# Causal attention in five steps a quad of heads instead of six

## The chip, the cores and the metric

One core of a Trainium2 chip runs the whole program. The metric is the device time of one execution in microseconds (us); the kernel before has a median of 998.64 us over three runs (998.04 to 999.71). Engines: PE is TensorE (PEld its weight loads), DVE VectorE, ACT ScalarE, POOL GpSimd, SP SyncE, which only issues DMAs here.

## The reference, cut to what matters

`x` has 4 sequences of 512 positions with 128 features. Six sub-layers follow one another, and attention, in 16 heads of 8, is part of four of them:

```
x = x + 0.5 * L0_ffn(layernorm(x))    # full attention, then the best of 8 experts
x = x + L0_attn(layernorm(x))         # causal attention
x = x + 0.5 * L0_ffn(layernorm(x))    # the same weights again
x = x + 0.5 * L1_ffn(layernorm(x))    # two dense low-rank-corrected experts
x = x + L1_attn(layernorm(x))         # causal attention
x = x + 0.5 * L1_ffn(layernorm(x))
```

An attention is softmax(q k^T / sqrt(8) + mask) v for each head, then a projection. In the causal ones a position sees itself and those before it, so of the 4 x 4 blocks of 128 x 128 scores of a head ten are needed, four of them masked along the diagonal. All of it is fp32 in the reference.

## The kernel before, in words

A *batch* here is one attention of one sequence: 16 of them, 0 to 3 and 8 to 11 full, 4 to 7 and 12 to 15 causal. A batch has four *quads* of four heads. Each quad is handled in two passes over its scores. `p1` (TensorE, L594, stationary q, moving k; for the diagonal blocks also mask products, L600) writes scores into a pair of PSUM banks, and VectorE takes the negated maximum of every row of every block (`blockm`, L948) and, after the last chunk, of every row (`negm`, L953). On POOL `split` (L1225 to L1231) writes that maximum as three bf16 parts. `m` (TensorE, L650) transposes them, ScalarE copies them out (`mrow`, L785), and two DMAs that SyncE issues (L1276) put them as extra rows into the stacked q, so that `p2` (L594 again, stationary k, moving q) computes score minus maximum. ScalarE writes the exponentials to `pt` (L795), and `pv` (TensorE, L675, fp32: each product is two records) multiplies them by the values and adds up in one bank. After every second quad `evac` (ScalarE, L801) copies that bank out, and `o` (L683) transposes it; after the fourth `onT` (L688) and `out` (L693) project the batch.

A *step* `(c, t)` is one chunk `c` of the scores for pair `t` of the quad's heads; the two heads of a pair (`s`) have a bank each. A causal quad has three chunks. c0 has the four diagonal blocks, c1 four full ones, c2 the two that are left: 512, 512 and 256 columns a head. So the six steps, 0 to 5, are (0,0), (0,1), (1,0), (1,1), (2,0), (2,1).

PSUM: two pairs of banks in turn for the "A" jobs (`p1`, `v`, `o`, `out`, ...), three banks in a ring for the "B" jobs (`p2` takes two of them, `hT`, `q`, `k`, `m`, `onT`, ... one each), and bank 7 for `pv`. A `p2` waits until every B bank taken before it but the last has been read; another B job until all but the last two have; an A job until all A jobs but the last have. `pt` is a ring of eight steps.

All engines run through one plan in order, made by `segment`, for three segments: batches 0 to 3, 4 to 11, 12 to 15. It goes through the steps of the second pass (a *slot* each). In a slot there come: the *jobs* whose time has come, counted in quads (so a slot of a causal quad begins at a sixth); what is due by slots; the first pass of the quad two ahead (`LEAD`); `p2`. Before the first quad two quads' `p1` alone are the segment's lead. After the last `p1` of a quad come `split` and, `M_LATER` = 4 slots later, `m`. After the second pair's `p2` of a chunk, `pv` is due `V_LATER` = 2 slots later for its first half (`VALUES`), 3 for its second. `evac`, `o`, `onT` and `out` are due 3, 5, 7 and 9 slots after a quad's last step. The jobs are the preparation of later batches (`PREP`, in quads before the batch: `hT` 6.967, `q` 6.767, `k` 6.486, `v` 2.951, with layer norm and remainders), the DMAs that stack the bf16 parts of q and k (`STACK`), and feed-forward work.

## Time and profile before

| | |
|---|---|
| runs | 998.04, 998.64, 999.71 us |
| profiled execution, span | 996.2 us |
| its own time | not listed apart; the runs' median is 2.4 us above its span |
| TensorE busy | 890.2 us (89%) |
| VectorE busy | 759.1 us (76%) |
| ScalarE busy | 674.5 us (68%) |
| GpSimd busy | 331.3 us (33%) |
| mean granted TensorE clock | 0.974 |
| causal batches 4 to 7 begin (their first `p2`) | 328.93 us |
| causal maxima (L948), first and last | 316.8 and 930.9 us |

The span is what lies between the first and the last instruction of one profiled execution; the runs' times have a little around it. The causal parts are about the slices 13 to 19 and 33 to 39 of the page's 40. A busy TensorE isn't one at its peak, since ends of products are modelled and products overlap.

### The profile page before, as it was taken

How to read it: one execution, taken by the hardware profiler on the slowest of the kernel's cores; microseconds unless marked ns; L12 is line 12 of the kernel's file. 1: busy time of each engine (PE TensorE's matmuls, PEld its weight loads, DVE VectorE, ACT ScalarE, POOL GpSimd, SP SyncE). 2: the span in 40 equal slices, each digit the busy share in tenths (PEclk: the TensorE clock that was granted, in tenths of full speed). 3: DMA queues.
4: the chain of work that ended last, by engine and by line, in shares of the span. 5: the costliest groups of instructions: out<-in, count | busy, mean ns of one | idle time of the engine just before them, and what ended most of it. 6: DMA issues, size and time to landing. Idle time of an engine off the chain costs nothing.

```text
span 996.2 us, 25709 instructions
## 1 busy us (share of the span) xinstructions
PE 890.2 (89%) x10020; PEld 474.5 (48%) x10020; DVE 759.1 (76%) x1352; ACT 674.5 (68%) x1470; POOL 331.3 (33%) x603
## 2 busy tenths in 40 slices
PE   2699999898888899999999998889798989999998
PEld 1123333235877455554323333249685545555565
DVE  5889999873536887888999999916347888888646
ACT  2388887687666677777798877786462367777631
POOL 4454312241655323332232412416651132311101
PEclk9699999999989999999999999999899999999999
DMA  4117740010133211111111100010310222110000
GB/s 145 51 35 189 189 108 13 16 34 22 39 112 107 63 51 43 46 51 40 34 45 31 44 18 2 24 42 31 98 57 1 64 66 57 43 38 5 3 22 22
DMA packets 60521, 52.32 MB, mean 53 GB/s; under 512 B 9106, under 2 KB 57362, under 8 KB 60402
## 3 DMA queue, kind: packets, MB, share of 16 engines
q1 hardware_dynamic: 48980, 40.00, 14.9%
q10 hardware_dynamic: 8478, 4.62, 2.1%
q0 software_dynamic: 2944, 6.05, 1.9%
q8 instruction: 81, 1.33, 0.6%
q14 instruction: 38, 0.31, 0.1%
HBM read 13.64 MB, written 11.06 MB: 25 GB/s over the span
## 4 chain that ended last, share of the span: by engine, by line
PE 57%; DVE 20%; ACT 10%; issue 7%; POOL 3%; DMA 2%; ACTq 1%; DVEq 0%; POOLq 0%; SPq 0%
PE ps L594 14%; PE ps L675 14%; DVE negm L957 10%; ACT pt L795 8%; PE ps L740 5%; PE ps L724 4%; PE ps L733 4%; DVE blockm L948 3%; PE ps L600 3%; PE ps L630 3%; PE ps L746 2%; PE ps L683 2%; PE ps L693 2%; PE ps L635 2%; DVE l_stats L992 1%
## 5 line engine op out<-in xcount | busy, mean ns | idle before, releaser
L795 ACT ACTIVATE pt<-ps 128x512 f32<-128x512 f32 (+1 forms) x896 | 458.2, 566 | 151.6 <-PE ps L594 101.5
L957 DVE TENSOR_REDUCE negm<-ps 128x2 f32<-128x1024 f32 x256 | 300.7, 1219 | 27.5 <-PE ps L594 25.5
L675 PE MATMUL ps<-pt,va 128*32 128x256 f32 (+1 forms) x4352 | 273.9, 340 | 11.8 <-ACT ot L801 5.0
L948 DVE TENSOR_REDUCE blockm<-ps 128x8 f32<-128x1024 f32 (+1 forms) x192 | 194.6, 1042 | 31.4 <-PE ps L594 20.1
L594 PE MATMUL ps<-ks,qs 61*128 61x128 bf16 (+2 forms) x1536 | 172.6, 291 | 31.4 <-DVE negm L957 17.3
L594 PE MATMUL ps<-qs,ks 64*128 64x128 bf16 (+3 forms) x1408 | 167.9, 295 | 6.1 <-ACT pt L795 2.0
L675 PEld LDWEIGHTS ps<-pt,va 128*32 128x32 f32 x4352 | 91.9, 108 | 125.0 <-issue 80.8
L594 PEld LDWEIGHTS ps<-ks,qs 61*128 61x128 bf16 x1536 | 54.5, 95 | 184.4 <-issue 85.6
L1225 POOL CAST mpart<-negm 128x16 bf16<-128x16 f32 x64 | 13.3, 209 | 296.3 <-DVE negm L957 153.6
L829 ACT ACTIVATE stage<-ps,pt 128x128 f32<-128x128 f32 x240 | 68.7, 371 | 30.5 <-PE ps L724 29.5
L594 PEld LDWEIGHTS ps<-qs,ks 64*128 64x128 bf16 x1408 | 57.9, 94 | 59.7 <-ACT pt L795 45.1
L1165 POOL TENSOR_TENSOR q<-q,parts 128x512 f32<-128x512 f32 x29 | 33.6, 1159 | 111.8 <-ACT parts L777 111.8
L724 PE MATMUL ps<-hTm,pt 128*128 128x128 f32 x480 | 67.6, 286 | 3.3 <-ACT stage L829 1.3
L733 PE MATMUL ps<-experts,stage 128*128 x480 | 65.1, 279 | 2.3 <-DVE pt L1077 2.2
L1077 DVE TENSOR_TENSOR pt<-ps,pt 128x128 f32<-128x128 f32 x60 | 17.2, 287 | 64.4 <-PE ps L733 63.3
L724 PEld LDWEIGHTS ps<-hTm,pt 128*128 128x128 f32 x480 | 61.4, 200 | 6.4 <-ACT stage L829 3.4
L733 PEld LDWEIGHTS ps<-experts,stage 128*128 128x128 f32 x480 | 59.0, 194 | 3.6 <-issue 3.4
L740 PE MATMUL ps<-hTa,wk 128*128 128x512 f32 x128 | 58.5, 599 | 0.9 <-ACT hTa L818 0.8
L1069 DVE COPY pt<-experts 128x644 f32 x60 | 32.1, 535 | 25.6 <-PE ps L675 23.5
L835 ACT ACTIVATE stage<-ps 128x512 f32<-128x512 f32 x32 | 19.1, 598 | 38.9 <-PE ps L740 37.5
L1260 POOL DMA_INDIRECT y_rows<-pt,stage x30 | 30.2, 1008 | 35.6 <-DVE pt L1077 29.0
L1089 DVE TENSOR_SCALAR stage<-ps,wpk 128x512 f32<-128x512 f32 x32 | 23.9, 747 | 22.9 <-PE ps L740 22.9
(150 smaller groups left out, 1062.7 us busy)
## 6 DMA issues: line engine op xcount, KB each, us to landing
qs<-parts SPq DMA_DIRECT2D x80, 128.0 KB
ks<-parts SPq DMA_DIRECT2D x77, 128.0 KB
experts<-in_experts SPq DMA_DIRECT2D x8, 578.0 KB, 5.5
sorted<-stage ACTq DMA_DIRECT2D x4, 967.5 KB, 8.4
qs<-mrow SPq DMA_DIRECT2D x128, 6.0 KB
pt<-y_rows SPq DMA_DIRECT2D x8, 256.0 KB, 3.1
qs<-parts SPq DMA_DIRECT2D x32, 56.0 KB
ks<-parts SPq DMA_DIRECT2D x30, 56.0 KB
```

Of the source, the lines that this page charges most:

```text
L594: ends[s] = pe.matmul(banks[s][:, col:col + c1 - c0], stationary[s][:, i * P:(i + 1) * P], moving[s][:, c0:c1], start=(m_ == 0), stop=(not ...
L675: ins = pe.matmul(pv_bank[32 * j:32 * j + 32, q0:q1], va[n % 2][:, kb, value_at(g, j):value_at(g, j) + 32], pt[:, k_, from_:from_ + q1 - q ...
L724: ins = pe.matmul(b_tiles(o)[:, a, :], we[:, number_of(n, at) % NWE, a * P:(a + 1) * P], hTm[:, number_of(n, at) % 2, :], start=True, stop ...
L733: ins = pe.matmul(pair_of(ka)[:, 0, 0:P], mid_e[:, number_of(n, at) % 2, a, :], w2.rearrange("p o c -> p (o c)"), start=(a == 0), stop=(a ...
L740: pe.matmul(pair_of(ka)[:, 0, :] if kx else b_bank(o), wk[:, kx, at * P:(at + 1) * P], hTa[:, n % 2, :], start=True, stop=True).then_inc(a ...
L795: a.activation(pt[:, k_ % NPT, S * s:S * s + width], b_bank(o + s)[:, 0:width], ACT.Exp).then_inc(b_free, 1)
L829: ins = a.activation(mid_e[:, number_of(n, at) % 2, fb, :], b_tiles(o)[:, fb, :], ACT.Relu, bias=we[:, at_, F + fb:F + fb + 1])
L948: v.tensor_reduce(blockm[:, g % 2, :, t, PLACES[c_]], pair_of(ka)[:, :, 0:width].rearrange("p s (b c) -> p s b c", c=P), AX, ALU.max, nega ...
L957: v.tensor_reduce(negm[:, g % 2, :, t, c_], pair_of(ka), AX, ALU.max, negate=True).then_inc(a_free, 1)
L1069: v.tensor_copy(we[:, number_of(n, at) % NWE, :], experts[:, bass.ds(expert[n, at], 1), 0:WE] .rearrange("p o c -> p (o c)")).then_inc(lai ...
L1165: eng.tensor_tensor(q32[:, c_, :], q32[:, c_, :], parts[:, c_, 0, :], ALU.subtract).then_inc(rem_done[c_], 1)
L1260: g_.indirect_dma_start(d["y_rows"][n], bass.IndirectOffsetOnAxis(sorted_rows[n % 2][:, at, P:ROW] .bitcast(U32), 0), ysb[:, r, :], None). ...
```

## The change

The last causal chunk, c2, is handled once for both pairs: the scores of pair 1 stand beside those of pair 0 in the same two banks, 256 columns further (`SHARED`). A causal quad has the steps (0,0), (0,1), (1,0), (1,1), (2,BOTH), in both passes. The maximum of the last is taken of the full 1,024 elements in one instruction, its exponentials of 512 columns in each of two, and its value products are one call of 256 columns instead of two of 128. A slot is a fifth of a causal quad; `M_LATER`, `V_LATER` and all job times keep their numbers. `evac`, `o`, `onT` and `out` are due 2, 4, 6 and 8 slots after a causal quad's last step, since the last value call has no second half. Full batches keep their eight steps. The diff, without the places that only pass both pairs' q and k on or look up the last step:

```diff
@@ -63,12 +63,15 @@
            [(0, 0, P, S), (2, 3 * P, 3 * P, S)],
            [(1, 0, 2 * P, S)]],
 }
+BOTH = 2
+STEPS = {False: [(c, t) for c in range(TB) for t in range(2)], True: [(0, 0), (0, 1), (1, 0), (1, 1), (2, BOTH)]}
+SHARED = 2 * P
 
 VALUES = {
     False: [[[(kb, 0, 0, S // 2)], [(kb, S // 2, S // 2, S)]] for kb in range(TB)],
     True: [[[(kb, kb * P, kb * P, (kb + 1) * P) for kb in (0, 1)], [(kb, kb * P, kb * P, (kb + 1) * P) for kb in (2, 3)]],
            [[(0, 0, P, 3 * P)], [(0, 2 * P, 3 * P, S), (2, 3 * P, 3 * P, S)]],
-           [[(1, 0, 2 * P, 3 * P)], [(1, P, 3 * P, S)]]],
+           [[(1, 0, 2 * P, S)]]],
 }
 
 PLACES = [slice(0, 16, 5), slice(11, 15), slice(7, 10, 2)]
@@ -189,8 +192,8 @@
 def segment(batches, causal_of, jobs):
 
     quads = [(n, g) for n in batches for g in range(4)]
-    nstep = [2 * len(PASS1[causal_of[n]]) for n, _ in quads]
-    pass1 = [(n, g, c, t) for n, g in quads for c in range(len(PASS1[causal_of[n]])) for t in range(2)]
+    nstep = [len(STEPS[causal_of[n]]) for n, _ in quads]
+    pass1 = [(n, g, c, t) for n, g in quads for c, t in STEPS[causal_of[n]]]
     jobs = list(jobs)
     for k, n in enumerate(batches):
         if k == 0:
@@ -221,22 +224,24 @@
             n, g, c, t = pass1[done1]
             out.append(("p1", n, (g, c, t)))
             done1 += 1
-            if (c, t) == (len(PASS1[causal_of[n]]) - 1, 1):
+            if (c, t) == STEPS[causal_of[n]][-1]:
                 out.append(("split", n, g))
                 due.append((slot + M_LATER, "m", n, g))
         if own:
             Q, i = own
             n, g = quads[Q]
-            out.append(("p2", n, (g, i // 2, i % 2)))
-            if i % 2:
-                for half in range(2):
-                    due.append((slot + V_LATER + half, "pv", n, (g, i // 2, half)))
+            c, t = STEPS[causal_of[n]][i]
+            out.append(("p2", n, (g, c, t)))
+            if t:
+                for half in range(len(VALUES[causal_of[n]][c])):
+                    due.append((slot + V_LATER + half, "pv", n, (g, c, half)))
                 if i == nstep[Q] - 1 and g % 2:
-                    due.append((slot + V_LATER + 1, "evac", n, g // 2))
-                    due.append((slot + V_LATER + 3, "o", n, g // 2))
+                    last = V_LATER + len(VALUES[causal_of[n]][c]) - 1
+                    due.append((slot + last, "evac", n, g // 2))
+                    due.append((slot + last + 2, "o", n, g // 2))
                     if g == 3:
-                        due.append((slot + V_LATER + 5, "onT", n, None))
-                        due.append((slot + V_LATER + 7, "out", n, None))
+                        due.append((slot + last + 4, "onT", n, None))
+                        due.append((slot + last + 6, "out", n, None))
         slot += 1
     at = len(quads)
     while due or jobs:
@@ -585,14 +592,16 @@
 
             return VW * (8 * (g % 2) + 4 * (g // 2) + j)
 
-        def score_pieces(pe, pieces, diagonal, banks, stationary, moving, mask):
+        def score_pieces(pe, pieces, diagonal, t, banks, stationary, moving, mask):
 
 
             ends = [None, None]
-            for m_, (i, col, c0, c1) in enumerate(pieces):
+            pieces = [(u, i, col + SHARED * u * (t == BOTH), c0, c1) for u in ((0, 1) if t == BOTH else (t,))
+                      for i, col, c0, c1 in pieces]
+            for m_, (u, i, col, c0, c1) in enumerate(pieces):
                 for s in range(2):
-                    ends[s] = pe.matmul(banks[s][:, col:col + c1 - c0], stationary[s][:, i * P:(i + 1) * P],
-                                        moving[s][:, c0:c1], start=(m_ == 0),
+                    ends[s] = pe.matmul(banks[s][:, col:col + c1 - c0], stationary[s][:, u, i * P:(i + 1) * P],
+                                        moving[s][:, u, c0:c1], start=(m_ == 0),
                                         stop=(not diagonal and m_ == len(pieces) - 1), skip_group_check=True)
             for half in range(2 if diagonal else 0):
                 for s in range(2):
...
                 elif name == "pv":
                     g, c_, half = at
                     odd, pieces = g % 2, VALUES[w["causal"]][c_][half]
                     need(pe, a_free, at_a[("v", n, None)] + 1)
-                    need(pe, b_free, at_b[("p2", n, (g, c_, 1))] + 2)
+                    shared = (c_, BOTH) in STEPS[w["causal"]]
+                    need(pe, b_free, at_b[("p2", n, (g, c_, BOTH if shared else 1))] + 2)
                     if not odd and c_ == 0 and half == 0:
                         need(pe, pv_free, at_evac[(n, g // 2)])
                     for m_, (kb, col, q0, q1) in enumerate(pieces):
                         begins = not odd and c_ == 0 and half == 0 and m_ == 0
                         ends_ = odd and ev == final_pv(n, g) and m_ == len(pieces) - 1
                         for j in range(4):
-                            k_ = at_step[("p2", n, (g, c_, j // 2))] % NPT
-                            from_ = S * (j % 2) + col
+                            k_ = at_step[("p2", n, (g, c_, BOTH if shared else j // 2))] % NPT
+                            from_ = S * (j % 2) + SHARED * (j // 2) * shared + col
                             ins = pe.matmul(pv_bank[32 * j:32 * j + 32, q0:q1],
                                             va[n % 2][:, kb, value_at(g, j):value_at(g, j) + 32],
                                             pt[:, k_, from_:from_ + q1 - q0], start=begins, stop=bool(ends_),
@@ -789,7 +799,7 @@
                     need(a, x_moe, 8 if n >= 12 else 4 if n >= 4 else 0)
                     if k_ >= NPT:
                         need(a, pv_done, pv_of_step[k_ - NPT] + 1)
-                    width = max(col + q1 - q0 for _, col, q0, q1 in PASS2[w["causal"]][c_])
+                    width = SHARED * (t == BOTH) + max(col + q1 - q0 for _, col, q0, q1 in PASS2[w["causal"]][c_])
                     for s in range(2):
                         need(a, b_full, o + s + 1)
                         a.activation(pt[:, k_ % NPT, S * s:S * s + width], b_bank(o + s)[:, 0:width],
@@ -944,10 +954,14 @@
                     g, c_, t = at
                     need(v, m_parts, 4 * (at_quad[(n, g)] - 1))
                     if w["causal"]:
-                        width = max(col + k1 - k0 for _, col, k0, k1 in PASS1[True][c_])
-                        v.tensor_reduce(blockm[:, g % 2, :, t, PLACES[c_]],
-                                        pair_of(ka)[:, :, 0:width].rearrange("p s (b c) -> p s b c", c=P), AX, ALU.max,
-                                        negate=True).then_inc(a_free, 1)
+                        if t == BOTH:
+                            v.tensor_reduce(blockm[:, g % 2, :, :, PLACES[c_]],
+                                            pair_of(ka).rearrange("p s (t b c) -> p s t b c", t=2, c=P), AX, ALU.max,
+                                            negate=True).then_inc(a_free, 1)
+                        else:
+                            v.tensor_reduce(blockm[:, g % 2, :, t, PLACES[c_]],
+                                            pair_of(ka).rearrange("p s (b c) -> p s b c", c=P), AX, ALU.max,
+                                            negate=True).then_inc(a_free, 1)
                         if ev == final_p1(n, g):
                             need(v, a_free, ka + 1)
                             v.tensor_reduce(negm[:, g % 2].rearrange("p s t i -> p (s t i)"),
```

## Rows read from the trace of the kernel before

**Rows 1.** Groups by line and form, 345 to 460 us: busy us, mean ns | idle before.

```profile
L948 DVE TENSOR_REDUCE blockm<-ps 128x8 f32<-128x1024 f32 x49 | 58.8, 1221 | 7.8 <-PE ps L594 3.9 <-POOL mpart L1225 1.7 <-PE ps L600 1.2
L948 DVE TENSOR_REDUCE blockm<-ps 128x4 f32<-128x512 f32 x26 | 17.7, 690 | 6.9 <-PE ps L594 6.7
```

**Rows 2.** Busy us by stretch: PE, PEld, DVE, ACT, POOL, granted clock, DMA share, GB/s.

```profile
348.80:385.54 36.74, 35.60 (x637) 20.29 (x633) 30.36 (x51) 28.43 (x64) 10.43 (x24) 1.00 0.18 47
920.00:940.00 20.00, 19.69 (x271) 10.13 (x264) 13.98 (x22) 13.37 (x29) 2.94 (x9) 1.00 0.01 3
```

**Rows 3.** Timeline, TensorE: start us, us, line, tiles, count [idle before <-releaser].

```profile
338.55 0.39 PE L594 MATMUL ps<-qs,ks 64*128 64x128 bf16 x8
...
357.14 0.39 PE L594 MATMUL ps<-qs,ks 64*128 64x128 bf16 x8
...
360.26 0.10 PEld L650 LDWEIGHTS ps<-identb,mpart 128*48 128x48 bf16 x1 [0.38 <-ACT pt L795]
...
361.34 0.39 PE L594 MATMUL ps<-qs,ks 64*128 64x384 bf16 x4
...
361.66 0.64 PE L675 MATMUL ps<-pt,va 128*32 128x128 f32 x16
...
362.90 0.64 PE L675 MATMUL ps<-pt,va 128*32 128x256 f32 x8 [0.20 <-ACT pt L795]
...
363.80 0.65 PE L675 MATMUL ps<-pt,va 128*32 128x128 f32 x16
...
364.83 0.39 PE L594 MATMUL ps<-qs,ks 64*128 64x128 bf16 x8
...
367.95 0.24 PE L650 MATMUL ps<-identb,mpart 128*48 128x128 bf16 x1
...
368.44 0.64 PE L675 MATMUL ps<-pt,va 128*32 128x128 f32 x16 [0.25 <-ACT ot L801]
...
373.76 0.39 PE L594 MATMUL ps<-qs,ks 64*128 64x128 bf16 x8
...
377.12 1.12 PE L630 MATMUL ps<-hT,wpk 128*128 128x512 f32 x2
...
385.54 0.39 PE L594 MATMUL ps<-qs,ks 64*128 64x128 bf16 x8
...
```

**Rows 4.** The chain of waits, 361 to 373 us: start us, us, what.

```profile
...
365.44 0.36 PE ps L675 x8
...
370.41 0.57 PE ps L675 x16
...
371.31 0.57 PE ps L675 x8
...
```

**Rows 5.** Timeline, ScalarE, and SyncE for the issue at 361.46.

```profile
361.17 0.26 ACT L785 ACTIVATE mrow<-ps 48x128 bf16<-48x128 bf16 x1
361.46 1.55 SPq L1276 DMA_DIRECT2D qs<-mrow  x2
...
363.90 0.66 ACT L795 ACTIVATE pt<-ps 128x256 f32<-128x256 f32 x2 [0.50 <-PE ps L594]
...
366.82 1.08 ACT L795 ACTIVATE pt<-ps 128x512 f32<-128x512 f32 x2 [0.26 <-PE ps L600]
367.79 0.60 ACT L801 ACTIVATE ot<-ps 128x512 f32<-128x512 f32 x1
...
378.28 0.69 ACT L775 ACTIVATE q<-ps,bcols 128x512 f32<-128x512 f32 x1
```

**Rows 6.** DMA, 361 to 365 us in 40 slices: tenths busy, GB/s.

```profile
DMA  0021002000000000000200000011000005997952
GB/s 0 10 51 21 0 0 82 0 0 0 0 0 0 0 0 0 0 0 13 46 3 0 0 0 0 0 26 36 0 0 0 0 0 133 195 184 215 338 174 92
```

**Rows 7.** Timeline of all engines, 325.3 to 329.2 us, a segment's first quad.

```profile
325.70 0.26 ACT L785 ACTIVATE mrow<-ps 48x128 bf16<-48x128 bf16 x1
...
328.93 0.51 PE L594 MATMUL ps<-qs,ks 64*128 64x128 bf16 x6
```

More of the change, by code:

```diff
@@ L496, in program @@
                 _, n, (g, c_, half) = ev
-                for t in range(2):
-                    pv_of_step[at_step[("p2", n, (g, c_, t))]] = len(at_pv)
+                for c, t in STEPS[causal_of[n]]:
+                    if c == c_:
+                        pv_of_step[at_step[("p2", n, (g, c, t))]] = len(at_pv)
                 at_pv[ev] = len(at_pv)
@@ L538, in final_p1 @@
         def final_p1(n, g):
-            return "p1", n, (g, len(PASS1[causal_of[n]]) - 1, 1)
+            return ("p1", n, (g, *STEPS[causal_of[n]][-1]))
         def final_p2(n, g):
-            return "p2", n, (g, len(PASS2[causal_of[n]]) - 1, 1)
+            return ("p2", n, (g, *STEPS[causal_of[n]][-1]))
         def final_pv(n, g):
-            return "pv", n, (g, len(PASS2[causal_of[n]]) - 1, 1)
+            c = len(VALUES[causal_of[n]]) - 1
+            return ("pv", n, (g, c, len(VALUES[causal_of[n]][c]) - 1))
         def round_before(n, r):
@@ L642, in pe_program @@
                     rows = [slice(HALF * s, HALF * s + ROWS) for s in range(2)]
-                    ends = score_pieces(pe, PASS1[w["causal"]][c_], w["causal"] and c_ == 0,
+                    ends = score_pieces(pe, PASS1[w["causal"]][c_], w["causal"] and c_ == 0, t,
                                         [pair_of(ka)[:, s, :] for s in range(2)],
-                                        [qs[n % NQK][rows[s], 2 * g + t, :] for s in range(2)],
-                                        [ks[n % NQK][rows[s], 2 * g + t, :] for s in range(2)], mask_q)
+                                        [qs[n % NQK][rows[s], 2 * g:2 * g + 2, :] for s in range(2)],
+                                        [ks[n % NQK][rows[s], 2 * g:2 * g + 2, :] for s in range(2)], mask_q)
                     ends[1].then_inc(a_full, 1)
@@ L655, in pe_program @@
                     rows = [slice(HALF * s, HALF * s + ROWS + MROWS) for s in range(2)]
-                    ends = score_pieces(pe, PASS2[w["causal"]][c_], w["causal"] and c_ == 0,
+                    ends = score_pieces(pe, PASS2[w["causal"]][c_], w["causal"] and c_ == 0, t,
                                         [b_bank(o), b_bank(o + 1)],
-                                        [ks[n % NQK][rows[s], 2 * g + t, :] for s in range(2)],
-                                        [qs[n % NQK][rows[s], 2 * g + t, :] for s in range(2)], mask_k)
+                                        [ks[n % NQK][rows[s], 2 * g:2 * g + 2, :] for s in range(2)],
+                                        [qs[n % NQK][rows[s], 2 * g:2 * g + 2, :] for s in range(2)], mask_k)
                     for s in range(2):
```

## The prediction

> **What bounds the kernel now.** I read the groups by line first, then the busy time by stretch, then the engines' timelines of single quads. The change touches the exponentials (ACT L795), the score maxima (DVE L948, in two sizes) [rows 1], the value products (PE L675) and the score products (PE L594). In a whole causal batch of 36.74 us TensorE is busy 35.60 us, VectorE 30.36 and ScalarE 28.43, at a granted clock of 1.00 [rows 2]: TensorE is the bound by its busy time. But a busy PE includes the modelled tail of each product, so I look for what it queues behind. One batch is four quads, and they differ. I measure a quad from the first second-pass score product of its first step (call it S0) to that of the next. D, 348.80 to 357.14, has the output transposes `o` (L683); A, to 364.83, has nothing but its own steps; B, to 373.76, has `o` and `onT` (L688); C, to 385.54, has the next batches' `hT`, `v`, `q`, `k` and the projection `out`. So D = 8.34, A = 7.69, B = 8.93, C = 11.78 [rows 2, 3], together the 36.74.
>
> One chain stands in every quad. Step 1's exponentials end on ScalarE (366.82 + 1.08 = 367.90 in B), TensorE transposes the row maxima (`m`, L650) 0.05 later, and the value products follow; in A it is `m` at 360.26, released by an exponential too [rows 3, 5]. From S0 to `m` it is 3.12 us in A and in B (364.83 to 367.95) [rows 3]. From `m` to the next S0 it is 4.57 us in A [rows 3]. In this second part lies a DMA that nobody waits for today: ScalarE copies `m` into `mrow` at 361.17, SyncE issues its two DMAs at 361.46, and S0 at 364.83 reads what they bring [rows 3, 5].
>
> **The change, part by part.** Six steps a quad become five; the last, c2, carries both pairs. The multiplications are the same: p1 and p2 keep every product and column. What goes:
>
> *TensorE.* In the chain a value call of 8 records of 128 columns takes 0.36 us, one of 16 takes 0.57 and 8 of 256 columns take 0.57 [rows 4]. So 8 records of 128 columns cost 0.215, and each call has 0.14 on top. After a step's score products some 0.13 more pass. Before, six runs of value products pay 0.27; afterwards there are four (the call for c2 directly follows c1's second, and step 2 has none): TensorE's own need falls by 2 x 0.27 = 0.54 a quad.
>
> *ScalarE and VectorE.* Exponentials cost 1.08 us per pair of 512 columns and 0.66 per pair of 256 [rows 5]. 4 x 1.08 + 2 x 0.66 becomes 5 x 1.08, but back-to-back starts are 0.49 and 0.28 apart, so it is 0.14 a quad less at most. The reductions: four of 1.22 and two of 0.69 become five of 1.22 [rows 1]; 0.16 less. The new reduction's input is contiguous and its output merely strided, so I take the time of the old 1,024-element form; the nearest rows bound it by 1.22 and twice 0.69, 1.38. These two engines aren't the bound in a causal batch, and the edit counts nothing there.
>
> *Where the value calls go.* They fall due two and three steps after their chunk. Before, each step had one. Afterwards: step 0 has c1's first half, step 1 c1's second half and then c2's single call, step 2 none, steps 3 and 4 c0's halves. Step 1's value products grow from 0.36 to 0.57 + 0.43 = 1.00, so its exponentials start 0.645 later. Step 2 has less to do, but its p2 waits for a bank of step 1's exponentials and `m` waits for the second one, so `m` stays 0.05 behind their end. S0 to `m` therefore grows from 3.12 to 3.765 in A, B, D. That is the price.
>
> *What it buys.* From `m` to S0 one step falls out. In A: `m` to step 4's value call 1.40 (360.26 to 361.66) [rows 3], value products 0.57, the double p1 0.22 and p2 0.22, turn 0.13: 2.54. The next value call needs step 3's exponentials: p2 at +1.08, exponentials 0.42 later, 1.08 long, 0.04 until PE starts: 2.62. Step 0 to S0 is 1.03 (363.80 to 364.83). Sum 3.65 instead of 4.57. Without another limit A = 3.765 + 3.65 = 7.42.
>
> *But `m` is now close to its reader.* It keeps its due time of four steps after `split`, which puts it at the start of step 3 as before; only two steps, no longer three, lie between it and S0. `mrow` is copied 0.91 after `m`, behind step 2's exponentials (360.26 to 361.17), and this stays. How long from the copy's start until S0 may run isn't shown, as nothing waits for it. Bounds: the packets of the second 6 KB move between 363.6 and 363.8, 2.63 after the copy's start [rows 6], and it can't be sooner; at 325.70 a copy starts and its S0 runs 3.23 later, at 328.93, right behind the mask products [rows 7], so it can't usually be later. I take 3.15, nearer to the upper end, because the completion still follows the packets. Then `m` to S0 is at least 0.91 + 3.15 = 4.06 and A = 3.765 + 4.06 = 7.83: 0.13 slower than before.
>
> The Trainium skill, "DMA: Bandwidth & Descriptors", section on the anatomy of one DMA, gives a fixed cost of about 2.0 us a transfer, mostly the receipt of the last write. From the second issue (halfway in the 1.55 us row at 361.46) that would be 3.07 after the copy's start, so A would be 7.75; the packets' row agrees that most of it lies behind the issue.
>
> *B and D.* After an odd quad the copy of `pv` (`evac`, 0.60, 367.79) stands before step 2's exponentials, and the value products wait for it until 368.44 [rows 3, 5]. It is now due in step 1, where ScalarE has room between 2.75 and 3.3 us of the cycle; it is gone from the path. `m` to S0: A's 3.65 + `o` 0.59 = 4.24, above 4.06, so the DMA is hidden. B without `onT`, and D: 3.765 + 4.24 = 8.01 instead of 8.34, -0.33. POOL's `split` and VectorE's `on` (read two steps later) have over 1 us of room.
>
> *C.* Jobs are placed by the quad's fraction: with fifths `q` stays in step 2 but `k` (1.51) moves from step 4 to step 3, before `m`. S0 at 0, `q` at 3.36 (373.76 to 377.12) + 0.645 = 4.01 [rows 3], `out` 4.97, p2 of step 2 at 6.18, `k` at 6.51, `m` 7.47, its value products 7.63. p2 of step 3 needs `k`'s bank: `k`'s two copies, 0.69 each as `q`'s at 378.28 [rows 5], overlap by 0.1 and run 7.6 to 8.87; `mrow` starts at 8.77, S0 is 3.15 later, 11.92 against 11.78: +0.14. SyncE: the stack DMAs go past `m` in its queue with the fractions, but it has been waiting for `mrow` each time, and keeps doing so. In the first C of a segment (338.55 to 348.80, 10.25 us, neither `v` nor `out`) [rows 2, 3] the same reckoning has q's copies end at 5.53, `k` 5.58, `mrow` 7.81, S0 10.96: +0.71.
>
> **Sum over 32 quads.** A 6 x 0.13 = +0.8; B 6 x -0.33 = -2.0; first quads of the two segments 2 x -0.2 (no `evac`, but a `v`; a guess between A and B); C 4 x 0.14 = +0.6 and 2 x 0.71 = +1.4; D 4 x -0.33 = -1.3; three quads of the last segment where VectorE has layer norms besides 3 x -0.16; two in which the following batch's full maxima bind VectorE, -0.1; the last three, where dense products fill TensorE (19.69 of 20 us [rows 2]) and the 0.54 counts, 2 x -0.54 and -0.1; two fewer reductions in each lead, -0.2. Together -2.9. The span of 996.2 becomes 993.3. It is 2.4 below the median of the runs, 998.64; I keep that distance: 995.7 us.
>
> **Rivals.**
> (1) *All of it arrives.* `m`'s DMA lands early enough (3.15 is too high, towards 2.63) and no wait replaces the old ones. Then A is 7.42 and C 11.5: -0.28, -0.33, -0.28, -0.33, or -1.2 a batch; with eight batches and the ends about -9.5: 989. For it: S0 has never been seen waiting for this DMA. Against: the two steps between.
> (2) *The 0.54 in full.* If the turn between forms of product alone limited, 32 x 0.54 = 17: 981.5. The row at 362.90, 0.20 idle behind an exponential, and the 0.25 behind `evac` speak against it. The Trainium skill, "TensorEngine Tiling (Array Packing)", key properties, says that changing the tiling mode drains TensorE, so fewer changes pay in full; the 0.14 a call agrees that a change costs, and the waits say that it isn't all.
> (3) *Slower: the DMA decides in every quad.* With each 0.1 us beyond 3.15 from copy to S0, A and C lose 0.1, and B and D too after their first 0.18. The batch stands at -0.39 with 3.15, at about zero from 3.33. The upper bound within a steady quad is 3.66 (361.17 to 364.83) [rows 3, 5]; at 3.5, A +0.48, C +0.49, B and D -0.16: +0.65 a batch, +5 less 2 at the ends: 1001.5. The stack DMAs on the same queue speak for it, as they would run into the short gap.
> (4) *Nothing moves*: `k`'s and `m`'s new places eat the 0.33 of B and D exactly; within 2 us of 998.64.
>
> **How the numbers follow.** Forecast 0.45, rival 1 0.17, rival 2 0.03, rival 3 0.18, rival 4 0.17. The forecast itself (993.5 to 998) lies by a quarter within 0.2% (2.0 us, what a measurement tells from no change). So faster 0.34 + 0.17 + 0.03 = 0.54, rounded down for slot effects that I can't see to 0.50; same 0.30; slower 0.20. The range 989.5 to 1001.5 leaves out rival 2 and the tails of 1 and 3.
>
> **What would show it.** Exponentials: 160 causal pairs, all 512 wide; 160 maxima of 1,024; value records in causal quads down from 72 to 64. A PE idle of 0.5 us before step 2's p2, none before the value call behind `evac`. In A the score products of S0 start right after the landing, 4.0 to 4.1 behind `m`, with PE idle before them; A near 7.8, B and D 0.3 shorter, C about the same. If S0 doesn't wait, rival 1 holds; if A is over 8.1, rival 3. An odd time for the 1,024-element reduction with its four-part output would make the forecast wrong in another way.

## The result, and the profile after

The changed kernel takes 1002.70 us (median of 5 runs, 1000.41 to 1004.24) against 999.34 for the kernel before (5 runs, 998.04 to 1000.17): ratio 1.0034, 95% interval 1.0020 to 1.0047. It is slower by a third of a per cent, where 995.7 us was forecast; the median lies 1.2 us above the top of the range. Each time is its execution's span and 1.8 us. The profiled execution of the changed kernel is the fastest of its five (span 998.6, 2.4 more than before); the other four have spans of 1000.1 to 1002.4 at a mean granted clock of 0.965 or 0.966 instead of its 0.969.

The page of the changed kernel: busy time by engine, a line of the chain that ended last (cut to whole lines), and groups with busy us, mean ns | idle before.

```profile
PE 875.8 (88%) x9764; PEld 473.6 (47%) x9764; DVE 756.9 (76%) x1320; ACT 671.6 (67%) x1406; POOL 331.1 (33%) x603
...
PE ps L603 12%; PE ps L685 11%; DVE negm L971 10%; ACT pt L805 9%; PE ps L750 5%; PE ps L734 4%; PE ps L743 4%; DVE blockm L962 3%; PE ps L756 2%; PE ps L639 2%; PE ps L609 2%; PE ps L693 2%; PE ps L703 2%; DMA qs<-mrow 2%; PE ps L644 1%
...
L805 ACT ACTIVATE pt<-ps 128x512 f32<-128x512 f32 x832 | 451.4, 596 | 154.7 <-PE ps L603 95.2
```

TensorE has 14 us less to do, VectorE 2 and ScalarE 3, and the span is 2.4 longer: what was saved has gone into waits. The list of lines now has a releaser that the same list of the kernel before doesn't have, the DMA of `mrow`, with 2% of the span. (Lines move: L594 is now L603, L600 L609, L650 L659, L675 L685, L785 L795, L795 L805, L948 L962 and for c2 L958, L1276 L1290.)

Groups by line and form of the changed kernel, 346 to 461 us, answering [rows 1]:

```profile
L962 DVE TENSOR_REDUCE blockm<-ps 128x8 f32<-128x1024 f32 x49 | 59.1, 1222 | 13.9 <-PE ps L609 8.0 <-PE ps L603 5.7
...
L958 DVE TENSOR_REDUCE blockm<-ps 128x8 f32<-128x1024 f32 x13 | 15.9, 1221 | 1.5 <-PE ps L603 1.5
```

The merged reduction costs the same 1.22 us as the others, as taken. Now quad A, TensorE's timeline in the changed kernel (start us, us), answering [rows 3]:

```profile
358.50 0.39 PE L603 MATMUL ps<-qs,ks 64*128 64x128 bf16 x8
...
361.79 0.39 PE L603 MATMUL ps<-qs,ks 64*128 64x384 bf16 x4 [0.47 <-ACT pt L805]
...
362.27 0.24 PE L659 MATMUL ps<-identb,mpart 128*48 128x128 bf16 x1
...
362.44 0.65 PE L685 MATMUL ps<-pt,va 128*32 128x128 f32 x16
...
366.36 0.40 PE L603 MATMUL ps<-qs,ks 64*128 64x128 bf16 x8 [0.26 <-DMA qs<-mrow]
```

And the chain of waits over the same stretch:

```profile
363.30 0.16 ACT mrow L795
...
364.28 1.95 DMA qs<-mrow
...
366.36 0.40 PE ps L603 x8
```

From S0 (358.50) to `m` it is 3.77 us (3.765 was reckoned), and from `m` to the next S0 4.09 (4.06). `mrow` is copied at 363.19, its DMA lands at 366.23 and S0 runs 0.13 later: 3.17 behind the copy's start, where 3.15 was taken. The named DMA is the releaser in A, and A takes 7.86 (7.83 forecast).

The Trainium skill, "DMA: Bandwidth & Descriptors", section on the anatomy of one DMA, gives about 2.0 us of fixed cost for a DMA issued from GpSimd. These are issued by SyncE; the chain's 1.95 from the second issue to the landing agrees.

The quads in the profiled executions, S0 to S0, in us (C1 is the first C of each causal segment, quads 17 and 49 of 64, counted from 0; "54" is quad 54, which stands in the last segment where a D would; f is the forecast):

| | A | B | C | D | C1 | 54 |
|---|---|---|---|---|---|---|
| before | 7.70 | 8.93 | 11.78 | 8.34 | 10.25 | 9.75 |
| changed (f) | 7.86 (7.83) | 8.51 (8.6) | 12.27 (11.92) | 7.93 (8.01) | 11.15 (10.96) | 10.76 (9.6) |
| m_late | 9.16 (10.7 in each segment's first) | 9.59 | 13.42 | 9.56 to 11.14 | 12.51, 15.09 | |
| m_early | 7.48 | 8.66 | 11.55 | 8.07 | 10.41 | 13.11 |
| pv_late | 7.47 | 8.47 | 12.41 | 7.88 | 10.67 | 10.75 |
| k_back | 7.86 | 8.51 | 11.81 | 7.92 | 10.39 | 14.31 |
| six_slots | 7.44 | 8.81 | 11.27 | 7.91 | 10.10, 10.53 | 10.77 |
| six_pv2 | 7.22 | 8.81 | 11.28 | 8.10 | 9.87 | 11.89 |

(B's 8.6 is the 0.33 taken off 8.93.) A whole steady batch went from 36.74 to 36.57: the merge pays a little there. The slowdown is elsewhere. Measured against forecast by terms of the sum (changed minus before, us):

| term | forecast | measured |
|---|---|---|
| A, B and D of steady batches | -2.5 | -3.0 |
| C, four later ones | +0.6 | +1.3 |
| C1, two | +1.4 | +1.8 |
| first quad of each segment | -0.4 | -0.1 |
| leads | -0.2 | +1.05 |
| quads 54, 57, 58 (VectorE's layer norms) | -0.5 | +1.0 |
| last two quads before the full batches | -0.1 | +0.6 |
| full batch 8, second quad | 0 | +1.0 |
| last three quads and the end | -1.2 | -1.2 |
| sum | -2.9 | +2.4 |

### The profile page after: what moved, and what is told of

It reads as the page before. It is cut to its first block, busy times and chain, and to the rows that moved or that the text cites. A ratio compares the mean times of both kernels' runs of the same rounds, so it can differ in the third digit from the quotient of the medians.

```text
span 998.6 us, 25098 instructions
## 1 busy us (share of the span) xinstructions
PE 875.8 (88%) x9764; PEld 473.6 (47%) x9764; DVE 756.9 (76%) x1320; ACT 671.6 (67%) x1406; POOL 331.1 (33%) x603
## 4 chain that ended last, share of the span: by engine, by line
PE 52%; DVE 20%; ACT 12%; issue 8%; POOL 3%; DMA 3%; ACTq 1%; SPq 0%; DVEq 0%; POOLq 0%
PE ps L603 12%; PE ps L685 11%; DVE negm L971 10%; ACT pt L805 9%; PE ps L750 5%; PE ps L734 4%; PE ps L743 4%; DVE blockm L962 3%; PE ps L756 2%; PE ps L639 2%; PE ps L609 2%; PE ps L693 2%; PE ps L703 2%; DMA qs<-mrow 2%; PE ps L644 1%
## 5 line engine op out<-in xcount | busy, mean ns | idle before, releaser
L805 ACT ACTIVATE pt<-ps 128x512 f32<-128x512 f32 x832 | 451.4, 596 | 154.7 <-PE ps L603 95.2
L685 PE MATMUL ps<-pt,va 128*32 128x256 f32 (+1 forms) x4096 | 260.5, 350 | 7.5 <-ACT ot L811 1.8
L603 PE MATMUL ps<-ks,qs 61*128 61x128 bf16 (+2 forms) x1536 | 168.4, 293 | 33.6 <-DVE negm L971 18.0
L603 PE MATMUL ps<-qs,ks 64*128 64x128 bf16 (+3 forms) x1408 | 162.8, 295 | 19.6 <-ACT pt L805 11.7
L962 DVE TENSOR_REDUCE blockm<-ps 128x8 f32<-128x1024 f32 x128 | 153.2, 1220 | 32.8 <-PE ps L609 21.3
L603 PEld LDWEIGHTS ps<-ks,qs 61*128 61x128 bf16 x1536 | 56.4, 95 | 184.7 <-issue 85.2
L685 PEld LDWEIGHTS ps<-pt,va 128*32 128x32 f32 x4096 | 88.9, 108 | 107.8 <-issue 68.6
L603 PEld LDWEIGHTS ps<-qs,ks 64*128 64x128 bf16 x1408 | 58.1, 95 | 72.9 <-ACT pt L805 54.1
L639 PE MATMUL ps<-hT,wpk 128*128 128x512 f32 x64 | 38.4, 687 | 3.9 <-ACT hT L778 1.8
```

Of the source, the lines that this page charges most:

```text
L603: ends[s] = pe.matmul(banks[s][:, col:col + c1 - c0], stationary[s][:, u, i * P:(i + 1) * P], moving[s][:, u, c0:c1], start=(m_ == 0), sto ...
L639: pe.matmul(b_bank(o), w["w" + name], hT[:, :], start=True, stop=True).then_inc(b_full, 1)
L685: ins = pe.matmul(pv_bank[32 * j:32 * j + 32, q0:q1], va[n % 2][:, kb, value_at(g, j):value_at(g, j) + 32], pt[:, k_, from_:from_ + q1 - q ...
L805: a.activation(pt[:, k_ % NPT, S * s:S * s + width], b_bank(o + s)[:, 0:width], ACT.Exp).then_inc(b_free, 1)
L962: v.tensor_reduce(blockm[:, g % 2, :, t, PLACES[c_]], pair_of(ka).rearrange("p s (b c) -> p s b c", c=P), AX, ALU.max, negate=True).then_i ...
```

## The experiments

All edits are to the changed kernel's plan, except where said. Each ratio is against runs of the kernel before that were made alongside, with medians of 998.50 to 999.49 us. k_back, lead_m and out_late have one run each, so their whole times decide nothing; they are read by their quads.

**m_late and m_early: is `m`'s DMA the new bound of a quad?** `m` one slot later, and one slot sooner.

```diff
-                due.append((slot + M_LATER, "m", n, g))
+                due.append((slot + (5 if causal_of[n] else M_LATER), "m", n, g))   # m_late; 3 in m_early
```

> The changed kernel with the maxima's transpose `m` due five slots after `split` in causal quads instead of four, so that one step instead of two lies between it and S0, the next quad's first second-pass product. If the two DMAs of `mrow` decide when S0 runs (theory 1), each plain quad (A, D) grows from 7.86 and 7.93 to about 9.3 us, since the copy's start moves from 0.9 to about 1.1 us behind a transpose that is itself 1.2 us later, and 3.18 follow; B grows by 0.8, and the time by 25 to 40 us. If the DMA is only seen waiting beside another limit (theory 2: the doubled value call of step 1; theory 3: the jobs that moved with the fifths), A grows by less than 0.5 us and the time by less than 8.

> The changed kernel with `m` due three slots after `split` in causal quads, at the start of step 2. It then needs no bank that step 1's exponentials hold; the copy follows those exponentials directly. Theory 1 (the DMA decides): quad A falls from 7.86 to about 7.5 us, D and B stay within 0.1, and S0 no longer starts right behind a landing; the time falls by 3 to 5 us below the changed kernel's, to about that of the kernel before. Theory 2 (the doubled value call decides): A stays above 7.8. Theory 3 (moved jobs): A stays, C (now 12.27) too. In a segment's lead `m` stands even further ahead among the first-pass products, where VectorE is the bound and POOL's parts aren't ready: up to 1 us lost there a segment by any theory.

m_late took 1049.70 us (2 runs, ratio 1.049, 1.046 to 1.053). TensorE in it, quad A from S0 at 407.00:

```profile
407.00 0.40 PE L603 MATMUL ps<-qs,ks 64*128 64x128 bf16 x8 [1.48 <-DMA qs<-mrow]
...
411.91 0.24 PE L659 MATMUL ps<-identb,mpart 128*48 128x128 bf16 x1
...
416.16 0.40 PE L603 MATMUL ps<-qs,ks 64*128 64x128 bf16 x8 [1.50 <-DMA qs<-mrow]
```

ScalarE's copy, and who waited for the DMA between 346 and 461 us (us in total, times, longest):

```profile
412.98 0.26 ACT L795 ACTIVATE mrow<-ps 48x128 bf16<-48x128 bf16 x1
```

```profile
PE ps L603 <- DMA qs<-mrow: 16.6, 11, 1.9
```

4.91 to `m`, 1.07 to the copy, 3.18 to S0: 9.16. The waits of 11 quads make 16.6 us, 1.51 each, and those of all 32 quads 46.0 us; the whole slowdown against the changed kernel, 47.0 us, is 1.47 a quad. B grew by 1.08 and the time by more than the 25 to 40 us expected, since every quad waits. The chain of `m`, copy, DMA and S0 bounds the quad, as in the forecast.

m_early has A at 7.48: S0 (366.51) comes 3.88 behind the copy, which is at 362.63, and no longer waits. B and D grew by 0.15 and 0.14 where at most 0.1 was expected.

```profile
359.03 0.39 PE L603 MATMUL ps<-qs,ks 64*128 64x128 bf16 x8
...
361.56 0.24 PE L659 MATMUL ps<-identb,mpart 128*48 128x128 bf16 x1
...
366.51 0.39 PE L603 MATMUL ps<-qs,ks 64*128 64x128 bf16 x8
```

Its steady batch is 35.76, almost 1 us under before; yet the whole took 1000.93 us (10 runs, ratio 1.0013, 1.0000 to 1.0027), 1.8 below the changed kernel and not 3 to 5. The first quad of a segment takes 11.08 instead of 9.57, quad 54 13.11, quad 58 11.21. So a steady quad's bound, though rightly named, wasn't what decides the sign.

**pv_late: the price in step 1.** c2's value call leaves step 1 for step 2, which had none; `evac` stays in time.

```diff
-                    due.append((slot + V_LATER + half, "pv", n, (g, c, half)))
+                    due.append((slot + V_LATER + half + (t == BOTH), "pv", n, (g, c, half)))
-                    due.append((slot + last, "evac", n, g // 2))
+                    due.append((slot + V_LATER + 1, "evac", n, g // 2))
```

> The changed kernel with c2's one value call, and `evac` behind it, one slot later: in the empty step 2 instead of behind c1's in step 1. Theory 2 (the doubled call is the price): the exponentials of step 1 and `m` come 0.43 us earlier, S0 to `m` falls from 3.77 to about 3.34; A falls to 7.48 even with the DMA wait, which stays 4.14 from `m` to S0; B and D get the wait behind `evac` back (0.25) and fall by 0.1 only; C falls by 0.4. About 8 us below the changed kernel: 994 to 996, faster than before by 3 to 5. Theory 1 alone says the same of A and makes no other claim. Theory 3: no quad gets shorter than the same quad of the kernel before except by the merged instructions, and C stays above 12.

997.03 us (9 runs, ratio 0.9979, 0.9963 to 0.9995): faster than the kernel before. TensorE's timeline:

```profile
358.09 0.39 PE L603 MATMUL ps<-qs,ks 64*128 64x128 bf16 x8
...
361.43 0.24 PE L659 MATMUL ps<-identb,mpart 128*48 128x128 bf16 x1
...
365.57 0.40 PE L603 MATMUL ps<-qs,ks 64*128 64x128 bf16 x8 [0.27 <-DMA qs<-mrow]
```

S0 to `m` falls from 3.77 to 3.34, 0.43 as the forecast priced that call; S0 still waits for the landing. It helps A by 0.39 and B and D by 0.05. C loses 0.14 where 0.4 was to be gained, and the time is 1 us above the 994 to 996 expected.

**k_back: `k` in C.** The job `k` comes due one slot later, behind `m`, as it did before the change.

```diff
-... ('k', 6.486), ...
+... ('k', 6.35), ...
```

> The changed kernel with one job time moved: `k` of a third or later batch 6.35 instead of 6.486 quads ahead, so that it falls into step 4 again and not into step 3 ahead of `m`. Read by quads. If `k`'s two copies before the copy of `m` are what makes quad C late (S0 to `m` 7.81, then 1.26 to the copy, then the landing), C falls from 12.27 to between 11.5 and 11.9 us, `m` comes 1 us earlier in it, and S0 behind it no longer starts 0.13 after a landing. A, B and D stay within 0.03. If C stays above 12.1, its loss is in `hT`'s wait for VectorE's layer norm and in the doubled value call, and the DMA only takes over.

The first of the later Cs in the changed kernel (quad 21), in which `k` (L639 at 381.63) stands ahead of `m` and its copies ahead of `mrow`:

```profile
375.69 0.63 PE L633 MATMUL ps<-identf,lnx 128*128 128x128 f32 x4 [0.21 <-DVE lnx L927]
...
381.63 1.12 PE L639 MATMUL ps<-hT,wpk 128*128 128x512 f32 x2
...
382.69 0.24 PE L659 MATMUL ps<-identb,mpart 128*48 128x128 bf16 x1
...
383.95 0.26 ACT L795 ACTIVATE mrow<-ps 48x128 bf16<-48x128 bf16 x1
```

and k_back:

```profile
380.55 0.24 PE L659 MATMUL ps<-identb,mpart 128*48 128x128 bf16 x1
...
381.62 0.26 ACT L795 ACTIVATE mrow<-ps 48x128 bf16<-48x128 bf16 x1
...
382.11 1.13 PE L639 MATMUL ps<-hT,wpk 128*128 128x512 f32 x2
```

C falls to 11.81 and C1 to 10.39, and S0 behind C comes 3.98 behind the copy instead of 3.19: `k`'s place is what made them longer. One run gave 1000.50 us all the same; quad 54 took 14.31 in it.

**lead_m: the start of a causal segment.** `m` of a segment's first quad one lead slot later, that is after two first-pass products of the next quad and not after one.

```diff
-                due.append((slot + M_LATER, "m", n, g))
+                due.append((slot + M_LATER + (own is None and g == 0), "m", n, g))
```

> The changed kernel with `m` of each segment's first quad one lead slot later, behind one more first-pass product. In the changed kernel TensorE stands at this `m` until POOL has written the parts, and the first-pass products behind it start VectorE's next maximum 1.27 us late. If that is the 0.95 us by which batch 4 begins later than before (its S0 at 329.88 instead of 328.93), S0 comes back to 328.9 to 329.1, and nothing changes inside the quads. If S0 stays at 329.8, the lead is late for another reason (the two sums `yadd` ahead of the last maximum).

The changed kernel at the first causal start, all engines:

```profile
324.29 0.24 PE L659 MATMUL ps<-identb,mpart 128*48 128x128 bf16 x1 [1.89 <-POOL mpart L1245]
324.46 0.59 PE L603 MATMUL ps<-ks,qs 61*128 61x128 bf16 x8
...
325.51 1.23 DVE L962 TENSOR_REDUCE blockm<-ps 128x8 f32<-128x1024 f32 x1 [1.27 <-PE ps L609]
```

lead_m:

```profile
322.80 4.61 DVE L962 TENSOR_REDUCE blockm<-ps 128x8 f32<-128x1024 f32 x4
...
324.05 0.24 PE L659 MATMUL ps<-identb,mpart 128*48 128x128 bf16 x1 [0.75 <-POOL mpart L1245]
```

With a lead counted in steps and five of them in a quad, `m` comes one product sooner in TensorE's order. It stands there for POOL's parts 1.89 us, the products behind it stand too, and VectorE, which sets the pace of the lead, goes idle for 1.27. lead_m starts the segment at 328.90 (changed 329.88, before 328.93), its first quad takes 8.95 instead of 9.57, which wasn't expected, and the span is 996.1, one run of 997.89 us. Part of the difference between the starts arises ahead of the leads, whose first maxima begin at 316.81 before and 317.10 in the changed kernel. From a segment's first causal maximum to its S0 it is 12.13 and 12.14 us before, 12.78 and 12.38 in the changed kernel, and 12.02 and 12.04 in lead_m: with `m` in its place the leads are 0.1 shorter each, as forecast.

The first quad of the last segment (9.29; 8.87 in lead_m, but also 8.81 in out_late and pv_late, where `m` of the lead has the changed kernel's place) has one wait more in the changed kernel. The S0 that ends it waits 0.69 for a landing that comes 4.45 behind the copy, because SyncE is still issuing DMAs that stack k when `mrow` is copied at 811.58 (start us, us):

```profile
811.02 2.14 SPq L1347 DMA_DIRECT2D ks<-parts  x2
813.21 1.61 SPq L1290 DMA_DIRECT2D qs<-mrow  x2
```

From that issue to the landing it is 2.82, about as in quad A (2.76). Of rival 3, which had the stack DMAs on the same queue in mind, this much does occur, once.

**out_late: the full batch behind.** `out` of the last causal batch one slot later.

```diff
-                        due.append((slot + last + 6, "out", n, None))
+                        due.append((slot + last + 6 + (n == 7), "out", n, None))
```

> The changed kernel with `out` of batch 7, the last causal one of the middle segment, one slot later, where the kernel before had it: beside the layer norm of batch 10, and not a slot ahead of it. In the changed kernel the second quad of batch 8, a full batch that the change doesn't touch, lasts 14.66 us instead of 13.67, and TensorE's `hT` waits there for that layer norm on VectorE. If `out`'s slot is the cause, this quad is back at 13.67 and nothing else moves by more than 0.1 us. If it stays at 14.66, the shift comes from the first-pass products, of which batch 8's now stand elsewhere among the value calls.

VectorE and TensorE in the changed kernel, where S0 of that quad stands at 492.51:

```profile
490.71 0.69 DVE L993 TENSOR_TENSOR upd<-ps,wpk 128x512 f32<-128x512 f32 x1
...
492.75 1.11 DVE L927 TENSOR_SCALAR lnx<-x,a_mv,a_rstd 128x128 f32<-128x128 f32 x4
...
494.00 0.63 PE L633 MATMUL ps<-identf,lnx 128*128 128x128 f32 x4 [1.11 <-ACT pt L805]
```

and out_late, S0 at 493.44:

```profile
492.59 1.11 DVE L927 TENSOR_SCALAR lnx<-x,a_mv,a_rstd 128x128 f32<-128x128 f32 x4
...
493.61 0.68 DVE L993 TENSOR_TENSOR upd<-ps,wpk 128x512 f32<-128x512 f32 x1
493.84 0.63 PE L633 MATMUL ps<-identf,lnx 128*128 128x128 f32 x4
```

`out` one slot early puts its update on VectorE ahead of the layer norm that TensorE's next `hT` needs. `hT` comes 1.49 behind S0 in the one and 0.40 in the other; the quad takes 14.66 and 13.71 (before 13.67). The releaser that the row names, an exponential, isn't it: the last one that `hT` needs a bank of had ended at 492.90; the norm ends at 493.86. The whole took 1001.49 us in one run; quad 54 took 12.22 in it.

**six_slots and six_pv2: is it the merge or the timetable?** The second pass keeps five steps, but a causal quad keeps six slots, the last with no step of its own, so every job, `m`, `evac`, `o` and `out` has its old place. six_pv2 has c2's value call a slot later as well.

```diff
-    body = [(Q + i / nstep[Q], Q + (i + 1) / nstep[Q], (Q, i)) for Q in range(len(quads)) for i in range(nstep[Q])]
+    nslot = [6 if causal_of[n] else 8 for n, _ in quads]
+    body = [(Q + i / nslot[Q], Q + (i + 1) / nslot[Q], (Q, i) if i < nstep[Q] else None)
+            for Q in range(len(quads)) for i in range(nslot[Q])]
...
-                due.append((slot + M_LATER, "m", n, g))
+                due.append((slot + (5 if causal_of[n] else M_LATER), "m", n, g))
...
+                    due.append((slot + V_LATER + half + 1 * (t == BOTH), "pv", n, (g, c, half)))   # 2 * in six_pv2
...
+                    evac_, o_, onT_, out_ = (3, 6, 8, 10) if causal_of[n] else (3, 5, 7, 9)   # evac 4 in six_pv2
```

> The changed kernel's merged instructions in the old timetable: a causal quad has six slots again, the last without score products, so every job has its old place (`k` in step 4 again), `m` stays in step 3 with an empty slot more between it and S0 in which c1's first value call stands, c2's value call and `evac` are in step 1, `o`, `onT` and `out` where they were. If the merging is sound and only the timetable costs (theories 1 to 3 together), A is about 7.5, B 8.6, D 8.0 and C 11.4 to 11.6, 1.1 a batch below the kernel before, and the time 988 to 992. If the merged instructions themselves cost (theory 4: for instance the 1,024-element reduction with four-part output, or the products of two pairs in one bank), the time stays above 998 and the groups of those instructions are longer than the old ones.

> Like the six-slot version, with c2's value call and `evac` one slot later, in step 2. Step 1 then has no value call: S0 to `m` falls from 3.33 to about 2.8 us. From `m` to S0 the DMA keeps 4.11 in A: A falls from 7.44 to about 6.9. In B and D the value products wait behind `evac` again (0.25): 8.81 and 7.91 fall by 0.3. C falls by 0.3 to 0.5. Some 1.4 us a batch, 9 to 11 in all: 983 to 986. If ScalarE is the bound by then (5.85 us of exponentials and copies in A's 6.9, and 1.35 of jobs a quad besides), A stops at 7.1 and the gain is 4 to 6 us.

six_slots: 993.90 us (5 runs; 988 to 992 was expected), ratio 0.9938 (0.9918 to 0.9958). six_pv2: 991.23 (4 runs), 0.9930 (0.9908 to 0.9953). The intervals don't tell the two apart. six_pv2, quad A on TensorE:

```profile
357.25 0.39 PE L605 MATMUL ps<-qs,ks 64*128 64x128 bf16 x8
...
360.33 0.24 PE L661 MATMUL ps<-identb,mpart 128*48 128x128 bf16 x1
...
364.47 0.39 PE L605 MATMUL ps<-qs,ks 64*128 64x128 bf16 x8
```

S0 to `m` is 3.08 there and not 2.8, and the next S0 comes 3.20 behind the copy (361.27), 0.02 later than one that waits for the landing. The steady batch is 35.43 in six_slots and 35.41 in six_pv2, 1.3 below before. The same merged instructions give 0.6% in the old timetable and lose 0.3% in the new one. In six_pv2 A stays at 7.22, not 6.9, B at 8.81 (its S0 comes 4.48 behind the copy, so no landing holds it), and D rose to 8.10: its expectation of 983 to 986 was too good.

**mended5: three repairs of the five-slot plan** (pv_late, lead_m and out_late together).

> Five slots kept, with three repairs of the timetable together: c2's value call and `evac` a slot later, `m` of a segment's first quad one lead slot later, `out` of batch 7 a slot later. Added up from the single runs: span 995.4 with the value call alone, less 0.9 for the lead, less 1.0 for `out`: 993.5, a median of about 995.5, 3 us faster than before and 1 to 2 slower than the six-slot version, since C stays at 12.4 and the DMA wait of A and C stays. If the parts don't add up (a gain given back in the stretches where VectorE is the bound), the span stays above 994.8.

994.91 us (4 runs), ratio 0.9950 (0.9933 to 0.9966), as expected. Against six_slots it keeps the longer C (12.40).

**fill5 and fill6: the clock.** The granted clock has stretches at half (1.2 GHz instead of 2.4) at the causal starts: 3.4 us each before, 10.2 and 6.8 in the changed kernel. That is the whole fall of the mean clock from 0.974 to 0.969 (10.2 us more at half are 5.1 of 998.6). Filler products keep TensorE busy where it stood:

```diff
+                if name == "m" and n in (4, 12) and at == 0:
+                    filling = True
+                if name == "p2":
+                    filling = False
+                if filling and name in ("m", "p1"):
+                    for i in range(32 if name == "m" else 10):
+                        pe.matmul(pv_bank[:, 0:P], identb[:, :], identb[:, :], start=True, stop=True, skip_group_check=True)
```

> The changed kernel with filler products on TensorE in the lead of both causal segments: 32 bf16 products of 128 columns (identity by identity, into the value bank, which nobody reads before it is begun anew) ahead of the first quad's `m`, where TensorE now stands 1.89 us, and 10 ahead of each first-pass product behind it. In the changed kernel TensorE is granted half its clock from 324.5 to 334.6 us (10.2 us) and for 6.8 us from 802; before it was 3.4 us each. Theory: the late start of the segments and part of their first quads is the price of that clock, which falls where TensorE has stood idle. Then the half-clock stretches shrink to 3.4 us or vanish, the first second-pass product comes at 329.3 to 329.5 instead of 329.88 (the score products at 324.46 take 0.39 and not 0.59; the 1.27 us that VectorE stands before them only shrink to some 0.9), the first quad takes 9.0 instead of 9.57, and the span loses 1.0 to 2.0 us. Rival: the clock doesn't matter there, since VectorE's maxima set the pace (1.12 from product to product in both): less than 0.3 us, or slower by the fillers that stand in the way. Quads 18 to 32 stay as they are.

> The same fillers in the version with six slots a quad and c2's value call in step 2. There the clock is at half for 3.4 us at 329, 6.8 us at 796 and 3.4 us at 861. By the clock theory the first two vanish and the third stays: 0.5 to 1.5 us less than 991.2, and a mean clock 0.003 to 0.005 higher. By the rival 991.2 or a little more.

Busy us of PE, PEld, DVE, ACT, POOL, then granted clock, DMA share, GB/s, first the changed kernel, then fill5:

```profile
320.00:330.00 10.00, 5.94 (x69) 3.10 (x69) 8.70 (x10) 3.71 (x7) 5.32 (x8) 0.73 0.42 111
```

```profile
320.00:330.00 10.00, 9.77 (x157) 6.99 (x155) 8.43 (x10) 3.73 (x7) 5.31 (x8) 1.00 0.40 111
```

Both half-clock stretches are gone, the mean clock is 0.976, and nothing is won: 1003.11 us (6 runs, ratio 1.0035, 1.0021 to 1.0050), S0 of the segment at 329.79 instead of 329.88, its first quad 9.94 instead of 9.57. fill6 took 991.46 us (4 runs, 0.9915, 0.9894 to 0.9935), as six_pv2 did. The gain of 1 to 2 us that I expected isn't there, but the test isn't clean, since the fillers stand in the way themselves. Here is fill5, and then out_late, whose lead has the changed kernel's code:

```profile
324.47 0.73 PE L630 MATMUL ps<-identb 128*128 128x128 bf16 x10
325.13 0.40 PE L603 MATMUL ps<-ks,qs 61*128 61x128 bf16 x8
...
325.79 3.49 DVE L970 TENSOR_REDUCE blockm<-ps 128x8 f32<-128x1024 f32 x3 [1.53 <-PE ps L609]
```

```profile
325.57 0.40 PE L603 MATMUL ps<-ks,qs 61*128 61x128 bf16 x8
...
326.23 3.49 DVE L962 TENSOR_REDUCE blockm<-ps 128x8 f32<-128x1024 f32 x3 [0.87 <-PE ps L609]
```

Ten fillers put the product behind `m` 0.66 later, and VectorE is idle for 1.53 us instead of 1.27. In out_late the half clock began 7.9 us behind the first causal maximum, in the changed kernel 7.4, so that this product still ran at full clock. VectorE was idle for 0.87, and the lead took 12.38 instead of 12.78. So 0.40 us of the changed kernel's first lead is the half clock. Where VectorE isn't kept waiting it costs nothing: in lead_m, six_slots and six_pv2 the leads take 12.01 to 12.04 with TensorE at half clock for up to 4.1 us of them. fill5's leads take 12.67 each, and fill6's 12.51 where six_pv2 has 12.01 and 12.04. What the half clock costs in the first quads isn't shown.

The Trainium skill, "TensorE: Matmul & The Clock Gate", section of terms, reckons the penalty as the throttled time times (1 - K/N), here half of it. For the 17 us taken away in fill5 that would be 8.5 us, an estimate. The runs show no gain, and the delay by fillers that the rows above show is 0.66 a lead, far less than would hide it; so at the starts the rule gives too much.

In quad 54 TensorE sets the pace, and there the price can be read. out_late and the changed kernel have the same code in it:

```profile
872.00:874.00 2.00, 2.00 (x31) 1.22 (x29) 1.07 (x2) 1.33 (x3) 0.00 (x0) 0.57 0.67 180
```

```profile
872.00:874.00 2.00, 2.00 (x40) 1.29 (x40) 1.72 (x4) 1.66 (x4) 0.00 (x0) 1.00 0.69 178
```

Instruction by instruction the two agree within 0.1 us until the half clock begins, 8.6 us into the quad. With 3.4 us at half clock the quad takes 12.22, without 10.76: 1.46. six_pv2 has 3.4 us too, and 11.89, where fill6, whose fillers are elsewhere, has none, and 10.39: 1.50. By the rule it would be 1.7. k_back's 14.31 has 6.8 us and m_early's 13.11 has 3.4. So whether that quad meets the half clock differs between executions and plans, and 3.4 us of it are worth 1.5. The nearest other execution of the changed kernel has a span 1.5 us above the profiled one and a lower mean clock; that this quad is why isn't shown, as only one has a trace.

## Why the prediction was wrong

- *TensorE's need, step 1's price, ScalarE, VectorE*: right. S0 to `m` 3.77; all maxima 1.22; of the value products' waits for `evac`, 5.0 us in the whole of the kernel before, 1.8 are left.
- *The landing, 3.15*: right, 3.17 to 3.18 in A, B's end 0.77 free, D's 0.19 behind the landing, that is nearly bound too. Rival 3 gave 1001.5, close to the time measured, but not by its mechanism: the DMA didn't land later. S0 of quad 49 is the exception: its DMAs were issued late (shown under lead_m). Rival 1's "all of it arrives" is nearly what m_early shows in the steady quads, and not in the whole.
- *A, B, D*: -3.0 for -2.5. Right.
- *C*: right in sign and cause (k_back), 0.35 short. S0 to `m` was 7.81 and not 7.47: `hT` comes 0.81 behind S0 instead of 0.54, since it waits for the layer norm on VectorE (the row at 375.69). I had moved `q` and `k` with the fractions, but not the norm; that the shift by slots put it nearer is argued, not tried.
- *The step that failed* is the sum's terms for all that isn't a steady quad: "two fewer reductions in each lead, -0.2", the first quads at -0.2 each, "three quads of the last segment where VectorE has layer norms besides 3 x -0.16", "two in which the following batch's full maxima bind VectorE, -0.1", and no term for the full batch behind. They were priced by the work that goes, without writing out the order that fifths give there. Together they were -1.2 and came out +3.5, which is 4.7 of the miss of 5.3. For the leads and the middle segment's first quad the cause is shown (lead_m): `m` stands one product sooner in TensorE's order. Of the first lead, 0.40 is the half clock. What the last segment's first quad misses of its gain goes with the late landing of its DMA. For the full batch the cause is shown too (out_late).
- *What stays open in those terms.* For quad 54, +1.0, it is only argued: VectorE is bound by layer norms and maxima there, and the final fraction of a quad is longer in fifths. It isn't the clock, which is 1.00 there in both profiled executions. The C ahead of it, quad 53, fell from 12.59 to 12.27 at the same time, so the two together take 22.34 before, 23.03 changed and 22.22 in six_slots (11.45 and 10.77): most of the +1.0 stands in the old timetable as well, and what of it is displaced work stays open. The +0.6 of the two quads before the full batches is 0.48 in quad 30 (9.46 to 9.94) and 0.10 in quad 31. pv_late and mended5 have quad 30 at 9.51, so the slot of c2's value call makes 0.43 of it; six_slots has 9.49, but six_pv2 has 9.93, which I can't explain.
- *The last three quads*: right, though by another sum than mine: the gain of 1.3 lies in the last one and the stretch behind, whose cause I didn't test.
- *The distance from span to median*: I kept 2.4; it is 4.1 in the changed kernel, 1.7 of the miss of 7.0. The one execution with a trace is the fastest of the five, so the terms above explain the span of 998.6 and not the other four.

## What to carry to other kernels

When a change alters how many slots a unit of work has, everything counted in slots or fractions moves: write out the new order at every seam (lead, transition, other kind of batch, end), not only in the steady loop, or keep the old slots and leave one empty. A transposed result that returns by DMA needs its 4.1 us from transpose to reader; count the steps between before taking one out. A clock theory can be tested with fillers, but count what the fillers delay; two executions with the same code and the half clock in different places tell it more cleanly. In these runs half clock cost time where another engine or the chain waited for TensorE, and none in the leads where VectorE wasn't kept waiting.

## What the runs showed of the hardware that I had not expected

- From the start of the copy of `mrow` to its landing it was 3.02 to 3.07 us in most steady quads of every kernel; a waiting reader ran 0.13 later. Some quads stand out (3.22 and 4.45 in the changed kernel, up to 5.69 in m_late); the 4.45 had its DMAs issued 1.63 behind the copy's start instead of 0.28.
- Filling TensorE's idle time of 1.89 us at a start brought the granted clock from 320 to 330 us to 1.00 from 0.73, and the time didn't fall.
- Two plans with the same code in a stretch, one execution each: one met the half clock there and the other didn't, 12.22 against 10.76 us for one quad. In a lead, a half clock that began 0.5 us sooner cost 0.40.
